# Adjacency of 126 instead of 147 column chunks, with large counts in a side table

## What is computed

```python
def _cheb(src, dst, feat, lam, W, b, n):
    deg = jnp.clip(jax.ops.segment_sum(jnp.ones(src.shape[0], feat.dtype), dst, num_segments=n), 1.0)
    dinv = deg[:, None] ** (-0.5)
    re_norm = 2.0 / lam[0]
    def unnL(f):
        return jax.ops.segment_sum((f * dinv)[src], dst, num_segments=n) * dinv
    X0 = feat
    X1 = -re_norm * unnL(X0) + X0 * (re_norm - 1.0)
    ...
    Xi = -2.0 * re_norm * unnL(X1) + X1 * (2.0 * (re_norm - 1.0)) - X0
...
h = _cheb(src, dst, embedding, lambda_max, cheb_W, cheb_b, n)
h = _cheb(src, dst, h, lambda_max, cheb_W, cheb_b, n)
out = _gatv2(src, dst, h, gat_W_src, gat_b_src, gat_W_dst, gat_b_dst, gat_attn, n)
...
out = jax.ops.segment_sum(x[src], dst, num_segments=x.shape[0])   # layer 3
```

## Time and profile before

| | before |
|---|---|
| median of 3 executions | 15081.34 us (15080.33 to 15083.89) |
| the profiled execution | 15077.83 us |
| its span | 15076.1 us |
| TensorE matmul busy | 8004.8 us (53%) |
| VectorE busy | 5414.9 us (36%) |
| GpSimd busy | 7421.9 us (49%) |
| ScalarE busy | 1922.5 us (13%) |
| mean granted TensorE clock | 0.735 |

### The profile page before, as it was taken

The page is one execution under the profiler, slowest core; times in us unless marked ns, Lnnn a source line. Parts: engine busy times, 40 slices in busy tenths (PEclk is TensorE's granted clock), DMA queues, the critical chain, the costliest instruction groups (busy, mean ns, idle before and its releaser), DMA issues. The chain is left out here.

```text
span 15076.1 us, 128768 instructions
## 1 busy us (share of the span) xinstructions
PE 8004.8 (53%) x48544; PEld 5313.2 (35%) x48544; DVE 5414.9 (36%) x8288; ACT 1922.5 (13%) x2243; POOL 7421.9 (49%) x7030
## 2 busy tenths in 40 slices
PE   3333332000001999999999200000089999999598
PEld 2333332000000444444444100000077777777344
DVE  5566666000001001010100233333278888888401
ACT  0000000000000000000000121121134444444000
POOL 5777777777776100101010577776665555553210
PEclk6555555555555999989999555555599999999799
DMA  4444543000001877868787111111111111111286
GB/s 163 163 157 167 177 158 128 3 0 0 0 0 48 294 286 274 294 218 298 263 294 271 28 44 38 38 44 32 25 27 30 36 30 32 34 30 30 102 298 248
DMA packets 516323, 1810.77 MB, mean 120 GB/s; under 512 B 218238, under 2 KB 299892, under 8 KB 407380
## 3 DMA queue, kind: packets, MB, share of 16 engines
q1 hardware_dynamic: 270628, 1547.76, 28.7%
q0 software_dynamic: 224288, 153.60, 5.5%
q10 hardware_dynamic: 20880, 101.97, 1.7%
HBM read 1425.63 MB, written 377.52 MB: 120 GB/s over the span
## 5 line engine op out<-in xcount | busy, mean ns | idle before, releaser
L189 POOL DMA_INDIRECT z_l<-table,idx_l x1568 | 1696.9, 1082 | 1299.8 <-DMA dir_p<-unit 805.2
L189 POOL DMA_INDIRECT g_l<-table_l,idx_l x1568 | 1950.5, 1244 | 508.9 <-issue 501.7
L1820 PE MATMUL p_r<-prod_k,ident 128*128 128x128 f32 x12544 | 1753.2, 284 | 182.8 <-DVE prod_k L2080 179.2
L793 POOL DMA_INDIRECT adj<-worth,sq x1568 | 1540.4, 982 | 566.1 <-issue 510.3
L189 POOL DMA_INDIRECT g_gat<-table,idx_gat x1568 | 1479.5, 944 | 513.6 <-issue 499.2
L1820 PEld LDWEIGHTS p_r<-prod_k,ident 128*128 128x128 f32 x12544 | 1607.6, 196 | 253.3 <-DVE prod_k L2080 221.0
L923 PE MATMUL p_h<-w_s,emb_s 10*128 10x16 f32 x3136 | 678.6, 369 | 1481.7 <-ACT hid L949 1088.5
L355 PE MATMUL pc_l<-spread,cross_lo 128*128 128x448 f32 x28 | 25.3, 1020 | 2243.9 <-DVE spread L359 2080.9
L923 PEld LDWEIGHTS p_h<-w_s,emb_s 10*128 10x128 f32 x3136 | 672.8, 327 | 1490.5 <-ACT hid L949 1091.4
L1456 PE MATMUL pr<-diag,ones 128*128 128x256 f32 x2 | 1.2, 712 | 2110.1 <-DVE diag L1474 2110.1
L2080 DVE TENSOR_TENSOR prod_k<-p_t,h_l 128x512 f32<-128x512 f32 x1568 | 1067.0, 680 | 0.0
(11 more groups left out here) (486 smaller groups left out, 12946.6 us busy)
## 6 DMA issues: line engine op xcount, KB each, us to landing
adj<-zeros SPq DMA_DIRECT2D x28, 8232.0 KB, 29.2
cells_cheb0a<-adj SPq DMA_DIRECT2D x168, 1344.0 KB, 5.8
cells_cheb0b<-adj SPq DMA_DIRECT2D x168, 1344.0 KB, 5.9
cells_cheb1a<-adj SPq DMA_DIRECT2D x168, 1344.0 KB, 5.7
cells_cheb1b<-adj SPq DMA_DIRECT2D x168, 1344.0 KB, 5.8
cells_l<-adj SPq DMA_DIRECT2D x168, 1344.0 KB, 5.8
gat_rows<-prod_gat ACTq DMA_DIRECT2D x28, 952.0 KB, 3.8
start_rows<-zeros SPq DMA_DIRECT2D x28, 896.0 KB, 4.1
```

The source lines that it names most:

```text
L189: return pool.indirect_dma_start(out=dest, out_offset=None, in_=table_ap, in_offset=bass.IndirectOffsetOnAxis(ap=index, axis=0))
L793: pool.indirect_dma_start(out=adj, out_offset=bass.IndirectOffsetOnAxis(ap=cell[:, t:t + 1], axis=0), in_=worth_u[:, t:t + 1], in_offset=N ...
L1820: last = nc.tensor.matmul(p_r[:], ident[:], prod_k[q % 2][:, :, :, k].rearrange("p g t w -> p (g t) w"), start=(k == 0), stop=(k == 15))
```

## The change

`GRP` becomes 56, so the first 56 edges of a destination go to its own column and a block has 56 edges: `BT` is 28, `CHUNKS` is 126, and a pass has ten full rounds and one of 6 chunks. `OV_R` is 2, the read back is in round 4, `BACK_R` is 6. Keys are compared up to 56 places apart: two calls of `count_shift` in each of the 28 steps and none behind the loop.

A cell holds counts up to `CAP` = 32. What a count has above 32 goes into a table of one number (`extra`) and one source row (`extra_i`) for each half block of `SUB` = 28 edges, `NS` = 56 a partition. It is made by seven operations on VectorE after the keys, with one load of the source rows. Each pass writes its features to `dense_rows` in DRAM (ScalarE's queue, first instruction), gathers 56 rows a partition of it on GpSimd, multiplies them by `extra` and adds them to the block sums before the scans, which now run over 56 half blocks; 56 instead of 49 rows are scattered.

```diff
-GRP = 32
-HL, HR = 64, 32
+GRP = 56
+SUB = 28
+CAP = 32
+HL, HR = 2 * GRP, GRP
...
-    assert BT * GRP == T
+    assert BT * GRP == T and GRP % SUB == 0 and SUB < CAP < GRP < 2 * CAP
+    NS = T // SUB
...
+        dense_rows = nc.dram_tensor("dense_rows", [ROWS, D], F32).ap()
...
# dense_pass
                     def _(act):
+                        act.dma_start(dense_rows.rearrange("(p j) f -> p j f", p=P), table_sb[:]).then_inc(rows_out, 16)
                         for r in range(N_R):
...
-                                act.wait_ge(over_out, at(over_out, 16 * BT))
+                                act.wait_ge(over_out, at(over_out, 16 * NS))
...
                     def _(pool):
+                        pool.wait_ge(rows_out, at(rows_out, 16))
+                        for t in range(NS):
+                            row_gather(pool, sums[:, t, :], dense_rows, extra_i[:, t:t + 1]).then_inc(extra_in, 16)
                         pool.wait_ge(over_summed, at(over_summed, 1))
-                        for t in range(BT):
+                        for t in range(NS):
...
+                                v.wait_ge(extra_in, at(extra_in, 16 * NS))
+                                link(V.tensor_tensor(sums[:], sums[:], by_col(extra[:]), ALU.mult))
+                                link(V.tensor_tensor(block_heads, block_heads, over[:], ALU.add))
                                 for f in range(D):
-                                    last = V.tensor_tensor_scan(over[:, :, f], osame[:], over[:, :, f], 0.0, ALU.mult, ALU.add)
+                                    last = V.tensor_tensor_scan(sums[:, :, f], osame[:], sums[:, :, f], 0.0, ALU.mult, ALU.add)
...
# l0_pass
-                    w = T + GRP - 1
+                    w = T + GRP
...
-                                count_shift(link, c + 1)
+                                link(count_shift(link, 2 * c + 1))
+                                count_shift(link, 2 * c + 2)
...
-                        for k in range(n_chunks + 1, SHIFTS + 1):
-                            link(count_shift(link, k))
-                        link(V.tensor_scalar(worth[:], later, 0.25, 0.25, ALU.mult, ALU.add, saturate=False))
-                        link(V.tensor_scalar(cell, repeat, 1.0, float(2 ** 28), ALU.min, ALU.mult))
+                        link(V.tensor_scalar(equal[:, 0:T], repeat, float(CAP - 1), 1.0, ALU.min, ALU.add))
+                        link(V.tensor_scalar(worth[:], equal[:, 0:T], 0.25, None, ALU.mult, saturate=False))
+                        link(V.tensor_scalar(cell, later, 1.0, float(2 ** 28), ALU.min, ALU.mult))
...
+                        link(V.tensor_scalar(excess, by_sub(repeat), float(1 - CAP), 0.0, ALU.add, ALU.max))
+                        link(V.scalar_tensor_tensor(excess, by_sub(later), 1.0, excess, ALU.is_lt, ALU.mult))
+                        link(V.tensor_reduce(extra[:], excess, AX.X, ALU.add))
+                        link(V.tensor_scalar(excess, excess, 1.0, None, ALU.min))
+                        v.wait_ge(s_in, at(s_in, 16))
+                        link(V.tensor_tensor(excess, src_i, excess, ALU.mult))
+                        link(V.tensor_reduce(cnt[:, 0:NS], excess, AX.X, ALU.add))
+                        link(V.tensor_copy(extra_i[:], cnt[:, 0:NS]))
```

More of the change, by code:

```diff
@@ L82, in gnn_kernel @@
     TX = HL + T + HR
-    KEYED = GRP - 1
     GROUPS = [(4 * g, min(4, NJ - 4 * g)) for g in range(-(-NJ // 4))]
@@ L140, in gnn_kernel @@
         sq = keep("sq", [P, NJ, D])
-        osame = keep("osame", [P, BT])
-        orow_i = keep("orow_i", [P, BT], I32)
+        osame = keep("osame", [P, NS])
+        orow_i = keep("orow_i", [P, NS], I32)
+        extra = keep("extra", [P, NS])
+        extra_i = keep("extra_i", [P, NS], I32)
         ocross_lo = keep("ocross_lo", [P, P])
@@ L179, in gnn_kernel @@
         over_summed = signal("over_summed")
+        rows_out = signal("rows_out")
+        extra_in = signal("extra_in")
         over_out = signal("over_out")
@@ L222, in prepare @@
                 oc = sb("oc", [P, 4])
-                orow = sb("orow", [P, BT])
+                orow = sb("orow", [P, NS])
                 mid = slice(HL, HL + T)
-                heads = slice(HL, HL + T, GRP)
+                heads = slice(HL, HL + T, SUB)
                 with nc.Block() as block:
@@ L486, in dense_pass @@
                 over = sb("over", [P, BT, D])
+                sums = sb("sums", [P, NS, D])
+                block_heads = sums[:].rearrange("p (t a) f -> p t a f", a=GRP // SUB)[:, :, 0, :]
                 acc = [st.enter_context(nc.psum_tensor(f"acc_{tag}{b}", [P, RC * P], F32)) for b in range(2)]
@@ L565, in _ @@
                     def _(pool):
+                        pool.wait_ge(rows_out, at(rows_out, 16))
+                        for t in range(NS):
+                            row_gather(pool, sums[:, t, :], dense_rows, extra_i[:, t:t + 1]).then_inc(extra_in, 16)
                         pool.wait_ge(over_summed, at(over_summed, 1))
-                        for t in range(BT):
+                        for t in range(NS):
                             pool.indirect_dma_start(out=ov_rows, out_offset=bass.IndirectOffsetOnAxis(ap=orow_i[:, t:t + 1], axis=0),
-                                                    in_=over[:, t, :], in_offset=None, bounds_check=ROWS - 1,
+                                                    in_=sums[:, t, :], in_offset=None, bounds_check=ROWS - 1,
                                                     oob_is_err=False).then_inc(over_out, 16)
@@ L611, in _ @@
                                                 ocross_hi[:].rearrange("p (j a) -> p j a", a=1).to_broadcast([P, NJ, D]),
-                                                over[:, BT - 1:BT, :].to_broadcast([P, NJ, D]), ALU.mult).then_inc(over_summed, 1)
+                                                sums[:, NS - 1:NS, :].to_broadcast([P, NJ, D]), ALU.mult).then_inc(over_summed, 1)
                         v.wait_ge(turned_free, at(turned_free, len(STEPS)))
@@ L729, in l0_pass @@
                 zero_dest = start_rows.rearrange("(p t) f -> p (t f)", p=P)
-                LINKS = 32
+                LINKS = 34
                 n_chunks = T // CH
@@ L736, in l0_pass @@
                 adj_fill = adj_flat.rearrange("(p c a n) -> p c a n", p=P, c=n_chunks, a=REP)
-                SHIFTS = GRP - 1
+                assert GRP == 2 * n_chunks
+                src_i = rows[0][:, :, 0:28].bitcast(I32)
+                excess = rows[1][:, :, 0:28]
                 worth_u = worth[:].bitcast(U8)
                 def count_shift(link, k):
-                    w = T + GRP - 1
-                    link(nc.vector.tensor_tensor(equal[:, 0:w], key[:, HL - GRP + 1:HL + T].bitcast(F32),
-                                                 key[:, bass.ds(HL - GRP + 1 + k, w)].bitcast(F32), ALU.is_equal))
-                    nc.vector.tensor_tensor(later, later, equal[:, GRP - 1:w], ALU.add)
-                    return nc.vector.tensor_tensor(repeat, repeat, equal[:, bass.ds(GRP - 1 - k, T)], ALU.add)
+                    w = T + GRP
+                    link(nc.vector.tensor_tensor(equal[:, 0:w], key[:, HL - GRP:HL + T].bitcast(F32),
+                                                 key[:, bass.ds(HL - GRP + k, w)].bitcast(F32), ALU.is_equal))
+                    nc.vector.tensor_tensor(later, later, equal[:, GRP:w], ALU.add)
+                    return nc.vector.tensor_tensor(repeat, repeat, equal[:, bass.ds(GRP - k, T)], ALU.add)
                 with nc.Block() as block:
@@ L775, in _ @@
                                     sp.dma_start(emb_s[u % 2][:], emb_t[:, bass.ds((c * CH + u * CS) * P, CS * P)]).then_inc(h_in[u % 2], 16)
+                        sp.wait_ge(keys_made, 1)
+                        sp.dma_start(src_i, src_rows.rearrange("p (h s) -> p h s", s=SUB)).then_inc(s_in, 16)
                         sp.wait_ge(zero_out, 16 * (T // CH + 2))
@@ L968, in l0_pass @@
             close(s_v, 1 + 2 * n * LINKS + final[0])
+            close(s_in, 16)
             close(s_pool, 2)
```

15 lines of the change are left out of this document (8 added, 7 removed).

## The result

| | before | after |
|---|---|---|
| median | 15080.83 us (4 executions, 15079.12 to 15083.89) | 14805.07 us (4 executions, 14785.64 to 14812.23) |
| the profiled execution | 15077.83 us | 14804.26 us |
| its span | 15076.1 us | 14802.5 us |

The ratio is 0.9814, 95% interval 0.9803 to 0.9826. The kernel is faster, by 276 us, about half of the 533.6 us that I forecast; the time lies above the whole range of 14495 to 14625 us.

What follows compares the result with a forecast made beforehand. TensorE was taken to bound the dense passes, GpSimd the layer 0 loop and counts. Passes -559.0, loop +31.6, rest -10.3 + 2.9 + 1.2 gave -533.6 us: median 14548 us, 0.965 of before, range 14495 to 14625.

Steps and rivals of the forecast that it cites:

- The step that failed: Pass start: 56 GpSimd gathers beside the loads of cells cost 0; 6 us a pass if they starve the loads.
- Rival 4: Passes: reads hitting one row make gathered rows late, holding up TensorE; 15249 us at 8 us a gather; 2%.
- Rival 3: Pass start: write goes ahead of first slice, gathers hold up loads; 7.8 + 6 us a pass, 14617 us; 8%.
- two rounds of 66.05 us gone: Each dense pass: two full rounds of 66.05 us disappear, part of the -116.8 us a pass.
- last round: End of each pass: last round has 6 chunks instead of 3 and takes 34.7 us instead of 19.37.
- first matmul: Pass start: 9 to 10 us after the first load instead of 6.0; the write's sharing costs 3.8 us.
- the scatter: Inside each pass: 56 rows take 75 us, ending about 296 us in; hidden, 34 us of slack.
- The loop term: Layer 0 loop: 28 more shifts each cost GpSimd 1.13 us, +31.6 us; bounds 0 and 105.
- VectorE's wait for rows: Sign in the layer 0 loop: the wait for gathered rows is near 19 us a step, before 22.02.
- The side table beside the writes: Behind the layer 0 loop: seven VectorE operations beside 1568 GpSimd writes cost +2.9 us; bounds 0 and 9.6.
- Rivals 1, 2 and 5: 1: GpSimd stands still per shift, 14622 us, 7%; 2: 256-column matmuls cost 0.216 us, 14599, 8%; 5: load-bound round, 14648, 3%.

Runs made afterwards that it cites:

- e1: Changed kernel, but each unused side-table entry (number 0) names a row of its own instead of row 0: 14555.58 us, 0.9645 of before.
- e2: Changed kernel without the side table's gathers; VectorE sets `sums` to zero instead, the write of the features stays: 14558.14 us, 0.9649 of before.
- e4: Against e1: unused entries name row 224 x t, one row for each gather, another for each of the 56: 14560.04 us, single execution.
- e14: The changed kernel as it is, on a slower chip where the kernel before takes 17295.94 us: 17200.6 us.

## Why the prediction was wrong

- **The step that failed** is "The 56 gathers ... take 8.3% of the DMA engines while they run, and 0.81 + 0.08 stays below 1 ... cost 0", with its bound of 6 us a pass. The 8.3% was read from gathers of different rows. With 56 gathers of one row the share was 53.5% (82.0% with nothing beside them), TensorE waited for loads inside the pass, and the first pass lost 53.0 us (788.2 against 735.2), the whole kernel 251.5 between the spans. The arithmetic would have held for different rows: e1 and e2 are the same.
- **Rival 4 saw the cause and missed the effect.** It said that 128 reads of a gather hit one row and that no row of the trace shows that, and then priced only the lateness of the gathered rows, from 5.4 us a gather on. They were not late: each landed within 51.4 us of its issue, and VectorE used them at 5156.2 us, 193 us after the last was issued. The harm was done to the loads, which share the engines. A cost that no row shows should have been carried into the sum's bounds through every resource it holds, not through one.
- **Rival 3 had the wait and not its size.** Its second half, gathers that hold up loads, is what came, but priced by the same 8.3% at 6 us a pass: about 49 us by the first copies (123.8 against 74.9 in e1), and 4.1 in the second round. Its first half, a write that goes ahead of the first slice, didn't come: 3.6 us, not 11.6.
- **Right for each pass:** two rounds of 66.05 us gone; last round 34.44 us (34.7); first matmul 9.65 us after the first load (9 to 10); the scatter, one round earlier in time, hidden. With the hot row gone the pass shrinks by 112.4 us (111.8).
- **The loop term was mis-sized:** 1.13 us a shift, measured 1.5. In the earlier trace rows I compared two gathers with two; the third, 1.38 us long at 1080.09, was stretched as well. From 1076.46 to 1081.77 three take 5.31 us where three undisturbed ones take 3.75: +1.56, and the three are one shift. So 28 x 1.5 = 42, not 31.6. VectorE's wait for rows fell from 22.0 to 19.5 us a step (forecast near 19).
- **The side table beside the writes:** the first pass starts 33.5 us later and the first count 32.0, so 1.5 us for it (2.9).
- **Added up again** with the two terms corrected: -533.6 + 10.4 (loop) + 251.5 (hot row) = -271.7 us; the spans differ by -273.6, the medians by -275.8.
- **Rivals 1, 2 and 5 didn't come:** a shift is 1.5 us and not 3.76, the last round shrank, no round behind the second got longer.

The version with own rows (e1) beats both: 14555.58 us, 0.9645 of before, where the changed kernel is at 0.9814.

## What to carry to other kernels

An index that stands for "nothing here" is still a read. When a gather is padded, give the unused entries rows of their own (in e4 one row for each gather was enough; two and eight rows were run only on the slower chips), never one common row, and look at what an index list holds before taking another gather's DMA share for it. And when a new transfer is weighed against slack, ask which engines it holds and who else needs them, not only when its own data are due.

## What the runs showed of the hardware

- Gathers of 128-byte rows, DMA engine time for a packet of four rows: where the kernel before takes 15080 us, 0.036 us with all rows different, 0.125 with one row for each gather, 0.58 when all gathers read one row (beside loads); on the slower ones 0.049 with all rows different, 0.042 with eight rows, 0.079 to 0.099 with two, 0.66 (beside loads) to 0.70 us (alone) with one row: 13.1 ns a read, 10 GB/s.
- With waits of 1.4 to 5.2 us between slices, two stretches of matmuls between them show a mean granted clock of 0.76 and 0.63 instead of 1.00; TensorE's longer busy time was 66 of the 251 us.
- A shift of three VectorE operations with two inputs each, 3.78 us in all, delays GpSimd's gathers by 1.5 us.
- On four of the five chips of the experiments TensorE got mostly one matmul in 2.8 us while GpSimd issued indirect DMAs (119.6 us instead of 66.05 for a round), and the same change was worth 95 us (one execution, e14) instead of 276.
